# Moving the third group's attention norm and projections out of the first feed-forward and into the job list of attention

## The chip, the cores and the metric

The kernel runs on one core of a Trainium2 chip. The metric is the device time of one execution in microseconds, and lower is better. Three runs of the kernel before took 278.95, 279.00 and 279.03 us, a median of 279.0. The profiled execution took 278.83 us, of which the span from the first to the last instruction is 277.1 us; 1.73 us lie around the span.

## What is computed

A block of three layers on x of shape 2 x 1024 x 128 (2048 tokens, 128 features), all in float32:

```python
x = x + 0.5 * ffn(layernorm(x))        # 8 experts of 128 -> 256 -> 128, gelu, all experts, one gate factor per token
x = x + attention(layernorm(x))        # a second layer norm with weights inside; 8 heads of 8, q and k of unit length
x = x + 0.5 * ffn(layernorm(x))

# attention, for each batch row b (1024 tokens) and each head
xn = layernorm(x) * ln_w + ln_b
q, k, v = split(xn @ w_qkv)            # 128 -> 3 x 64
sim = 8 * l2norm(q) @ l2norm(k).T      # causal
out = softmax(sim) @ v @ w_out
```

## The kernel before, in words

**Tokens.** The 2048 tokens are four groups of 512 (`GROUPS`, `GROUP`), numbered 0 to 3; a group is four tiles of 128. Groups 0 and 1 are batch row 0, groups 2 and 3 are batch row 1. "The third group" is number 2, `LAST` is number 3.

**First feed-forward (layer 0).** `ffn_group(0, g)` runs 16 chunks `c` for each group (L561 on TensorE, L877 on ScalarE, L1121 on VectorE, L1400 on GpSimd). A chunk is three matmuls up (L524, L527, L530), a gelu on ScalarE (L849, often again as a rounded copy at L852), a split on VectorE (L1021, L1023) and three matmuls down (L542, L545, L547). The tables `AT...` (L67 to L81) say in which chunk each side task sits. While group `g` runs, the side tasks prepare attention for group `g - 1`: statistics and norm on VectorE (`normalise`, L962), transposes on TensorE (`ln_transpose`, L479), the affine copy on ScalarE (`affine_features`, L795), and the projection to q, k and v (`qkv_products`, L612). For group `g - 2`: squares, copies, inverse lengths by Newton steps, unit vectors, 16-bit stacks, and the transposes of the stacks to `qT` and `kT`.

**What group 3 of layer 0 (the fourth) does at its end.** Transposes of group 2's norm at chunk 12 (L485), `qkv_products(2)` at chunk 13 (L623), the first scores and exponentials of attention between the last chunks, and on VectorE at chunk 15 `copy_k(1)`, `copy_qkv(2)`, `own_squares(2)`, `square_sums(2)`, `guesses(2)` (L1184 to L1189). After this `y_transposes(3)` (L549) waits for `qkv_copied` of group 2, because it writes a PSUM bank that the q, k, v products used; `residual` for group 3 follows on VectorE (L1321).

**Attention.** There are 40 loops `k` (L739), each a pair of steps: `scores(2k)`, `scores(2k+1)` on TensorE (L655), two exponentials on ScalarE (L862), masks of diagonal blocks on GpSimd (L1462), and `pv(k - 3)` on TensorE (L678). Scores go through three sets of PSUM banks, so `scores(s)` waits until the exponential of step `s - 3` has read its set. The loops go through four query groups (called pairs in the code): loops 0 to 5, 6 to 19, 20 to 25 and 26 to 39. Loops whose step is the last of a unit (2, 5, 12, 19, 22, 25, 32, 39) are half as wide. Query group 2 (loop 20 on) needs `qT` and `kT` of token group 2, and query group 3 (loop 26 on) those of group 3.

**Jobs.** Work that must share TensorE with attention is a list `jobs` (L254) of (at, kind, argument). TensorE fills a job's PSUM bank right after `pv(at)` (L765), so in loop `at + 3`; `fill(n)` first waits until job `n - 1` has been emptied (L689), and everything behind it in TensorE's order waits with it. VectorE empties the jobs in order (`empty`, L1263) in the loop at L1328, and between them does the tasks hung on each job by name. With `q1` = 6, `q2` = 20, `q3` = 26 the list before is:

```python
jobs = [(q1, "ln", LAST), (q1 + 1, "project", (0, 0)), (q1 + 2, "project", (0, 1)),
        (q1 + 5, "qkv", 0), (q1 + 6, "qkv", 1), (q1 + 7, "q_stack", LAST - 1), (q1 + 8, "k_stack", LAST - 1),
        (q1 + 12, "q_stack", LAST), (q2 + 1, "k_stack", LAST),
```

`output(pair)` (L1244) is VectorE's reading of a finished query group; it waits for that group's last `pv`. `inverse_lengths` (L359) is nine small dependent instructions for groups 2 and 3, `unit_vectors` (L383) two, `stacks` (L1106) four.

**Second feed-forward (layer 1).** It follows attention and is not touched.

Of the kernel before, what the change touches and what calls it, by code (L numbers as in the profile page):

```python
# [34 lines left out]
GROUP_TILES = 4  # L35
# [25 lines left out]
Q_GROUPS = SEQ // GROUP  # L61
TURNS = 2 * (GROUPS - 1)
# [41 lines left out]
def build(nc, x, ln_w, ln_b, w_qkv, w_out, gate_w, gate_b, rms_w, w1, b1, w2, b2, out):  # L104
# [9 lines left out]
    with ctx:  # L114
# [125 lines left out]
        for st in steps:  # L240
# [13 lines left out]
        jobs = [(q1, "ln", LAST), (q1 + 1, "project", (0, 0)), (q1 + 2, "project", (0, 1)),  # L254
                (q1 + 5, "qkv", 0), (q1 + 6, "qkv", 1), (q1 + 7, "q_stack", LAST - 1), (q1 + 8, "k_stack", LAST - 1),
                (q1 + 12, "q_stack", LAST), (q2 + 1, "k_stack", LAST),
# [86 lines left out]
        def qkv_banks(p):  # L343

            return (BANK_LN, BANK_QT) if p == LAST - 1 else (BANK_QT, BANK_KT)
# [37 lines left out]
        def unit_vectors(eng, p):  # L383
            if p < LAST:
                eng.wait_ge(qkv_copied, p + 1)
            else:
                eng.wait_ge(job_emptied, job_number["qkv", 1] + 1)
# [90 lines left out]
        def _(pe):  # L478
# [82 lines left out]
            def ffn_group(layer, g):  # L561
# [5 lines left out]
                for c in range(CHUNKS):  # L567
# [26 lines left out]
                    if operands and g >= 1 and c == at["att_transpose"]:  # L594
# [14 lines left out]
                    if operands and g >= 1 and c == at["att_qkv"]:  # L609
                        qkv_products(g - 1)  # L610

            def qkv_products(p):  # L612
# [3 lines left out]
                if p == LAST - 1:  # L616
                    pe.wait_ge(qT_done, p)
                else:
                    pe.wait_ge(gate_logits_done, p + 2)
                    pe.wait_ge(qT_done, p)  # L620
                    pe.wait_ge(kT_done, p)
# [37 lines left out]
            def pv(k):  # L659
# [6 lines left out]
                if opens and pair == 0:  # L666
                    pe.wait_ge(kT_done, LAST - 1)
# [16 lines left out]
            def fill(n):  # L684
# [11 lines left out]
                elif kind in ("ln", "ffn_ln"):  # L696
                    norm = ATT if kind == "ln" else FFN
                    pe.wait_ge(xn_done[norm], GROUP_TILES * (LAST + 1 if kind == "ln" else GROUPS + 1))
                    for i, tile in enumerate(tiles):
                        m = pe.transpose(bank[:, tile], xn[:, norm, i, :], ident[:, :])  # L700
                elif kind == "qkv":
                    for i in halves[arg]:
# [36 lines left out]
            for k in range(quad_steps + PV_LAG):  # L739
                if k < quad_steps:  # L740
# [37 lines left out]
        def _(act):  # L778
# [98 lines left out]
            def ffn_group(layer, g):  # L877
# [5 lines left out]
                for c in range(CHUNKS):  # L883
# [23 lines left out]
                    if operands and g >= 1 and c == at["att_copy"]:  # L907
# [37 lines left out]
        def _(dve):  # L945
# [142 lines left out]
            def copy_qkv(p):  # L1088
                dve.wait_ge(qkv_mm, p + 1)
                dve.wait_ge(qkn_done, 2 * p)  # L1090
                halves_qkv = [ps[:, bank, 0:384].rearrange("p (t c) -> p t c", t=2) for bank in qkv_banks(p)]
                for half, qkv in enumerate(halves_qkv):
                    dve.tensor_copy(qk_raw[:, 2 * half:2 * half + 2, :], qkv[:, :, 0:2 * INNER])
                for half, qkv in enumerate(halves_qkv):
                    for quad in range(QUADS):
                        last = dve.tensor_copy(v_of(slice(4 * p + 2 * half, 4 * p + 2 * half + 2), quad), v_columns(qkv, quad))
                last.then_inc(qkv_copied, 1)

            def own_squares(p):
                if p == LAST:  # L1100
                    dve.wait_ge(job_emptied, job_number["qkv", 1] + 1)
                else:
                    dve.wait_ge(qkv_copied, p + 1)
# [17 lines left out]
            def ffn_group(layer, g):  # L1121
# [7 lines left out]
                for c in range(CHUNKS):  # L1129
# [133 lines left out]
            def empty(n):  # L1263
# [9 lines left out]
                elif kind == "ln":  # L1273
                    dve.wait_ge(qkv_mm, LAST)
                    dve.tensor_scalar(xf[:, ATT, :], bank, cols[:, COL_LNW:COL_LNW + 1], cols[:, COL_LNB:COL_LNB + 1],
                                      ALU.mult, ALU.add).then_inc(job_emptied, 1)
                elif kind == "qkv":
                    dve.wait_ge(qkn_done, 2 * LAST)
                    qkv = bank[:, 0:384].rearrange("p (t c) -> p t c", t=2)
                    t0 = GROUP_TILES * LAST + halves[arg][0]  # L1280
# [210 lines left out]
```

## Time and profile before

| what | value |
|---|---|
| median of three runs | 279.0 us |
| profiled execution, its span | 278.83 us, 277.1 us |
| TensorE busy (matmul) | 266.6 us (96%) |
| ScalarE busy | 220.8 us (80%) |
| VectorE busy | 220.1 us (79%) |
| GpSimd busy | 76.2 us (27%) |
| first feed-forward | from the start to about 113 us |
| attention | about 109 to 180 us |
| granted TensorE clock | 1.000 over the span |

The shares are means over three layers with different limits; a stage has to be read by itself. In the rows of the trace, the first number is the start in us from the span's start, the second is how long the merged group of instructions took, and the bracket at the end is how long the engine had been idle and what ended the wait. A group that is not merged with the next still overlaps it a little: the step from one start to the next is what an instruction costs its engine.

### The profile page before, as it was taken

How to read it: one execution, taken by the hardware profiler on the slowest of the kernel's cores; microseconds unless marked ns; L12 is line 12 of the kernel's file. 1: busy time of each engine (PE TensorE's matmuls, PEld its weight loads, DVE VectorE, ACT ScalarE, POOL GpSimd, SP SyncE). 2: the span in 40 equal slices, each digit the busy share in tenths (PEclk: the TensorE clock that was granted, in tenths of full speed). 3: DMA queues.
4: the chain of work that ended last, by engine and by line, in shares of the span. 5: the costliest groups of instructions: out<-in, count | busy, mean ns of one | idle time of the engine just before them, and what ended most of it. 6: DMA issues, size and time to landing. Idle time of an engine off the chain costs nothing.

```text
span 277.1 us, 4946 instructions
## 1 busy us (share of the span) xinstructions
PE 266.6 (96%) x1627; PEld 182.1 (66%) x1627; DVE 220.1 (79%) x597; ACT 220.8 (80%) x343; POOL 76.2 (27%) x148
## 2 busy tenths in 40 slices
PE   8999999999999999899998999999999999999994
PEld 8676778887778787323333432277876887888782
DVE  7799989998988988966687355587988797687775
ACT  2888677868888788899999999977685868668672
POOL 7103004213850482452347332600400200200100
PEclk9999999999999999999999999999999999999999
DMA  4740000000000000000000000420004210301302
GB/s 154 211 114 1 0 1 2 0 1 0 2 1 0 5 0 0 2 0 2 1 2 0 4 0 2 102 52 0 1 1 114 39 38 2 77 2 36 78 1 76
DMA packets 21644, 7.80 MB, mean 28 GB/s; under 512 B 13458, under 2 KB 20852, under 8 KB 21620
## 3 DMA queue, kind: packets, MB, share of 16 engines
q1 hardware_dynamic: 21620, 7.50, 10.5%
q8 instruction: 13, 0.21, 0.3%
q14 instruction: 11, 0.09, 0.1%
HBM read 4.88 MB, written 2.62 MB: 27 GB/s over the span
## 4 chain that ended last, share of the span: by engine, by line
PE 75%; DVE 10%; ACT 7%; issue 7%; DVEq 0%; POOL 0%; ACTq 0%; POOLq 0%
PE ps L547 9%; PE ps L530 9%; PE ps L542 9%; PE ps L524 9%; PE ps L527 9%; PE ps L678 9%; PE ps L545 8%; ACT probs L862 4%; PE ps L655 3%; DVE h_lo L1023 2%; PE ps L717 2%; PE ps L709 2%; PE ps L633 1%; DVE h_hi L1021 1%; ACT h_hi L852 1%
## 5 line engine op out<-in xcount | busy, mean ns | idle before, releaser
L849 ACT ACTIVATE h<-ps,cols 128x512 f32<-128x512 f32 x128 | 87.9, 692 | 43.3 <-PE ps L530 40.1
L1023 DVE TENSOR_TENSOR h_lo<-h,h_hi 128x512 fp32r<-128x512 f32 x128 | 89.1, 701 | 17.5 <-ACT h_hi L852 15.0
L862 ACT ACTIVATE probs<-ps 128x1024 f32<-128x1024 f32 (+1 forms) x80 | 67.3, 1008 | 1.6 <-PE ps L655 1.4
L542 PE MATMUL ps<-h_hi,w_hi 128*128 128x512 f32 x128 | 52.2, 408 | 0.3 <-DVE h_hi L1021 0.3
L547 PE MATMUL ps<-h_lo,w_hi 128*128 128x512 f32 x128 | 51.1, 399 | 0.8 <-DVE h_lo L1023 0.7
L524 PE MATMUL ps<-xT_hi,w_hi 128*128 128x512 f32 x128 | 50.6, 396 | 0.0
L530 PE MATMUL ps<-xT_lo,w_hi 128*128 128x512 f32 x128 | 50.1, 392 | 0.2 <-DVE xT_lo L381 0.2
L852 ACT ACTIVATE h_hi<-ps,cols 128x512 fp32r<-128x512 f32 x73 | 49.9, 684 | 0.0
L545 PE MATMUL ps<-h_hi,w_lo 128*128 128x512 f32 x128 | 49.9, 390 | 0.0
L527 PE MATMUL ps<-xT_hi,w_lo 128*128 128x512 f32 x128 | 49.9, 390 | 0.0
L678 PE MATMUL ps<-probs,v_ones 128*32 128x512 f32 (+3 forms) x384 | 38.8, 495 | 0.3 <-POOL probs L1462 0.2
L1462 POOL TENSOR_SCALAR_AFFINE_SELECT probs<-probs 128x256 f32<-128x256 f32 x64 | 25.7, 428 | 34.3 <-ACT probs L862 33.4
L1372 POOL TENSOR_TENSOR gate_rms<-gate_ms,neg_half 128x4 f32<-128x4 f32 x8 | 10.6, 1321 | 82.6 <-DVE gate_ms L988 82.6
L547 PEld LDWEIGHTS ps<-h_lo,w_hi 128*128 128x128 f32 x128 | 24.0, 188 | 9.7 <-DVE h_lo L1023 5.0
L542 PEld LDWEIGHTS ps<-h_hi,w_hi 128*128 128x128 f32 x128 | 24.0, 188 | 7.0 <-issue 1.8
L1021 DVE CAST h_hi<-h 128x512 fp32r<-128x512 f32 x55 | 23.1, 421 | 6.3 <-ACT h L849 5.7
L530 PEld LDWEIGHTS ps<-xT_lo,w_hi 128*128 128x128 f32 x128 | 24.0, 188 | 6.0 <-DVE xT_lo L381 0.6
L524 PEld LDWEIGHTS ps<-xT_hi,w_hi 128*128 128x128 f32 x128 | 24.1, 188 | 5.1 <-issue 0.6
L527 PEld LDWEIGHTS ps<-xT_hi,w_lo 128*128 128x128 f32 x128 | 24.0, 188 | 5.0
L545 PEld LDWEIGHTS ps<-h_hi,w_lo 128*128 128x128 f32 x128 | 24.1, 188 | 4.2
L655 PE MATMUL ps<-qT,kT 32*128 32x512 f16 (+3 forms) x192 | 20.8, 329 | 2.5 <-ACT probs L862 2.1
L655 PEld LDWEIGHTS ps<-qT,kT 32*128 32x128 f16 x192 | 6.2, 91 | 24.4 <-ACT probs L862 15.2
(147 smaller groups left out, 265.9 us busy)
## 6 DMA issues: line engine op xcount, KB each, us to landing
w_raw<-in_L_ffn_w SPq DMA_DIRECT2D x8, 256.0 KB, 3.8
turned<-blocks SPq DMA_DIRECT2D x6, 256.0 KB, 2.0
w_raw<-turned SPq DMA_DIRECT2D x24, 64.0 KB, 2.4
x_sb<-in_L_attn_x SPq DMA_DIRECT2D x3, 256.0 KB, 7.4
out_x<-x_sb SPq DMA_DIRECT2D x3, 256.0 KB, 2.3
x_sb<-in_L_attn_x SPq DMA_DIRECT2D x2, 128.0 KB, 2.2
out_x<-x_sb SPq DMA_DIRECT2D x2, 128.0 KB, 1.9
wout_sb<-in_L_attn_w_out SPq DMA_DIRECT2D x8, 4.0 KB
```

The lines of the kernel that those rows point to most:

```text
L524: pe.matmul(bank, w1_hi[:, w], xT_hi[:, cols_g], start=True, stop=False)
L527: pe.matmul(bank, w1_lo[:, w], xT_hi[:, cols_g], start=False, stop=False)
L530: pe.matmul(bank, w1_hi[:, w], xT_lo[:, cols_g], start=False, stop=True).then_inc(up_done, 1)
L542: pe.matmul(y, w2_hi[:, w], h_hi[:, c % RING, :], start=(c == 0), stop=False)
L545: pe.matmul(y, w2_lo[:, w], h_hi[:, c % RING, :], start=False, stop=False)
L547: pe.matmul(y, w2_hi[:, w], h_lo[:, c % RING, :], start=False, stop=(c == CHUNKS - 1)).then_inc(down_done, 1)
L655: m = pe.matmul(ps[:, 2 * score_set(s) + hd, at:at + width], kT[rows, st["quad"], k0:k0 + P], qT[rows, st["quad"], qc:qc + width], start=T ...
L678: m = pe.matmul(ps[ROW * j:ROW * j + ROW, bank, q0:q0 + width], v_ones[:, SEQ // P * st["b"] + kt, 4 * st["quad"] + j, :], probs[:, (s + j ...
L849: first = nc.scalar.activation(h[:, slot, :], ps[:, BANK_H + slot, :], ACT.Gelu, bias=bias)
L852: nc.scalar.activation(h_hi[:, slot, :], ps[:, BANK_H + slot, :], ACT.Gelu, bias=bias).then_inc(gelu_done, 1)
L862: nc.scalar.activation(probs[:, s % P_SLOTS, :, 0:width], ps[:, bank:bank + 2, 0:width], ACT.Exp, scale=SCALE).then_inc(exp_done, 1)
L1023: dve.tensor_tensor(h_lo[:, slot, :], h[:, slot, :], h_hi[:, slot, :].bitcast(f32), ALU.subtract).then_inc(split_done, 1)
```

## The change

Group 2's share in attention leaves group 3 of the first feed-forward. `FIRST_JOB = 2` is the first token group whose norm transposes, affine copy and q, k, v products are jobs. Its statistics and `normalise` on VectorE stay where they are. In group 3 of layer 0 there is no `ln_transpose(ATT, 2)`, no `affine_features(2)` and no `qkv_products(2)`, and VectorE's block at chunk 15 keeps only `copy_k(1)`. The job list begins with group 2's ln and two qkv halves at `q1`, then the two output projections of query group 0 (two places later than before), then group 3's ln (six later), the stacks of group 2 (same place), group 3's qkv halves (four later), and group 3's q stack (one later). On VectorE, group 2's squares, sums and guesses hang on its second qkv job; its inverse lengths, unit vectors and stacks all hang on the second projection job; group 3's squares, sums, guesses, inverse lengths, unit vectors and stacks all hang on its second qkv job; `normalise(ATT, 3)` moves from ahead of `output(0)` to behind the first job, and `first_stats` of the second feed-forward hangs on group 3's ln job. The number of instructions for the arithmetic stays nearly the same; q, k and v of group 2 are now copied by job halves.

```diff
+FIRST_JOB = 2
@@ jobs
-        jobs = [(q1, "ln", LAST), (q1 + 1, "project", (0, 0)), (q1 + 2, "project", (0, 1)),
-                (q1 + 5, "qkv", 0), (q1 + 6, "qkv", 1), (q1 + 7, "q_stack", LAST - 1), (q1 + 8, "k_stack", LAST - 1),
-                (q1 + 12, "q_stack", LAST), (q2 + 1, "k_stack", LAST),
+        jobs = [(q1, "ln", 2), (q1 + 1, "qkv", (2, 0)), (q1 + 2, "qkv", (2, 1)),
+                (q1 + 3, "project", (0, 0)), (q1 + 4, "project", (0, 1)), (q1 + 6, "ln", LAST),
+                (q1 + 7, "q_stack", 2), (q1 + 8, "k_stack", 2), (q1 + 9, "qkv", (LAST, 0)), (q1 + 10, "qkv", (LAST, 1)),
+                (q1 + 13, "q_stack", LAST), (q2 + 1, "k_stack", LAST),
                 (q2 + 4, "project", (1, 0)), (q2 + 5, "project", (1, 1)),
...
@@ TensorE, y_transposes of the last group
-                    pe.wait_ge(qkv_copied, LAST)
+                    pe.wait_ge(qkv_copied, FIRST_JOB)
+                    pe.wait_ge(qT_done, 2)
@@ TensorE, ffn_group
-                    if operands and g >= 1 and c == at["att_transpose"]:
+                    if operands and 1 <= g <= FIRST_JOB and c == at["att_transpose"]:
...
-                    if operands and g >= 1 and c == at["att_qkv"]:
+                    if operands and 1 <= g <= FIRST_JOB and c == at["att_qkv"]:
                         qkv_products(g - 1)
@@ TensorE, pv and the attention loop
-                    pe.wait_ge(kT_done, LAST - 1)
+                    pe.wait_ge(kT_done, 2)
+                    pe.wait_ge(gate_logits_done, GROUPS)
...
-                            pe.wait_ge(qkv_copied, LAST)
+                            pe.wait_ge(resid, GROUP_TILES * LAST)
+                            pe.wait_ge(xf_done[ATT], FIRST_JOB)
                             pe.wait_ge(y_evac, GROUPS)
@@ ScalarE, ffn_group
-                    if operands and g >= 1 and c == at["att_copy"]:
+                    if operands and 1 <= g <= FIRST_JOB and c == at["att_copy"]:
                         affine_features(g - 1)
@@ VectorE, normalise
-                if n <= GROUPS:
+                if kind == ATT and n > FIRST_JOB:
+                    dve.wait_ge(job_filled, job_number["ln", n - 1] + 1)
+                elif n <= GROUPS:
                     dve.wait_ge(ln_t[kind], n)
@@ VectorE, ffn_group, chunk 15 of the last group
                         copy_k(g - 2)
-                        copy_qkv(g - 1)
-                        own_squares(g - 1)
-                        square_sums(g - 1)
-                        guesses(g - 1)
@@ VectorE, the job loop
-            inverse_lengths(dve, LAST - 1)
-            normalise(ATT, LAST, LAST)
             for n, (at, kind, arg) in enumerate(jobs[:-1]):
                 if n == 0 or pair_of_job(n) != pair_of_job(n - 1):
                     output(pair_of_job(n) - 1)
                 empty(n)
-                if kind == "ln":
-                    unit_vectors(dve, LAST - 1)
+                if (kind, arg) == ("ln", 2):
+                    normalise(ATT, LAST, LAST)
+                if (kind, arg) == ("qkv", (2, 1)):
+                    own_squares(2)
+                    square_sums(2)
+                    guesses(2)
                 if (kind, arg) == ("project", (0, 1)):
-                    stacks(LAST - 1)
-                    dve.wait_ge(job_emptied, n + 1)
+                    inverse_lengths(dve, 2)
+                    unit_vectors(dve, 2)
+                    stacks(2)
+                if (kind, arg) == ("ln", LAST):
                     first_stats(GROUPS)
-                if (kind, arg) == ("qkv", 1):
+                if (kind, arg) == ("qkv", (LAST, 1)):
                     own_squares(LAST)
                     square_sums(LAST)
-                if (kind, arg) == ("q_stack", LAST - 1):
                     guesses(LAST)
-                if (kind, arg) == ("k_stack", LAST - 1):
                     inverse_lengths(dve, LAST)
                     unit_vectors(dve, LAST)
                     stacks(LAST)
```

## Rows read from the trace of the kernel before

**Rows 1.** Busy time by stretch: us; PE, PEld, DVE, ACT, POOL busy (x); PEclk, DMA
```profile
127.00:142.00 15.00, 15.00 (x154) 5.90 (x156) 9.76 (x30) 14.86 (x18) 4.17 (x9) 1.00 0.01 2
```
**Rows 2.** Timeline of ScalarE: start, us, line, operation, count, idle before
```profile
107.06 0.77 ACT L798 ACTIVATE xf<-ps,cols 128x512 f32<-128x512 f32 x1
...
110.16 0.22 ACT L839 ACTIVATE gate_tanh<-gate_tmp 128x32 f32<-128x32 f32 x1
...
111.87 1.03 ACT L862 ACTIVATE probs<-ps 128x1024 f32<-128x1024 f32 x1 [0.58 <-PE ps L655]
...
114.79 33.62 ACT L862 ACTIVATE probs<-ps 128x512 f32<-128x512 f32 x40 [0.41 <-PE ps L655]
148.79 29.87 ACT L862 ACTIVATE probs<-ps 128x512 f32<-128x512 f32 x36 [0.38 <-PE ps L655]
```
**Rows 3.** Timeline of TensorE at the end of the first feed-forward
```profile
106.27 0.60 PE L485 MATMUL ps<-ident,xn 128*128 128x128 f32 x4
...
109.23 1.57 PE L623 MATMUL ps<-wqkv_sb,xf 128*128 128x192 f32 x8
...
113.91 0.63 PE L558 MATMUL ps<-ident,yT 128*128 128x128 f32 x4 [0.86 <-DVE v_ones L1096]
```
**Rows 4.** Timeline of VectorE, end of the first feed-forward and start of attention
```profile
109.53 0.19 DVE L999 TENSOR_TENSOR gate_tmp<-logits,gate_max 128x32 f32<-128x32 f32 x1
...
112.50 0.75 DVE L1093 COPY qk_raw<-ps 128x256 f32<-128x256 f32 x2
...
113.87 0.69 DVE L1104 TENSOR_TENSOR sq<-qk_raw 128x512 f32<-128x512 f32 x1
...
116.06 1.12 DVE L1058 SCALAR_TENSOR_TENSOR x_sb<-ps,gate_half,x_sb 128x128 f32<-128x128 f32 x4
...
118.42 0.19 DVE L366 TENSOR_TENSOR newton<-rnorm 128x64 f32<-128x64 f32 x1
...
119.96 0.37 DVE L366 TENSOR_TENSOR newton<-rnorm 128x64 f32<-128x64 f32 x1
...
120.98 1.52 DVE L967 TENSOR_SCALAR xn<-x_sb,mean_var,rstd 128x128 f32<-128x128 f32 x4
```
**Rows 5.** Timeline of GpSimd beside that
```profile
119.84 2.94 POOL L1462 TENSOR_SCALAR_AFFINE_SELECT probs<-probs 128x256 f32<-128x256 f32 x8
```
**Rows 6.** Timeline of VectorE, from the first finished query group on
```profile
124.36 0.72 DVE L1247 STREAM_TRANSPOSE o_blocks<-ps 128x512 f32<-128x512 f32 x1 [1.86 <-PE ps L678]
...
127.17 0.81 DVE L1275 TENSOR_SCALAR xf<-ps,cols 128x512 f32<-128x512 f32 x1 [0.51 <-PE ps L700]
```
**Rows 7.** Timeline of TensorE in attention: score, pv and job pieces of loops 10 to 15
```profile
128.39 0.71 PE L709 MATMUL ps<-wout_sb,o_feat 128*128 128x128 f32 x4
...
131.22 1.06 PE L678 MATMUL ps<-probs,v_ones 128*32 128x512 f32 x8
132.22 0.39 PE L655 MATMUL ps<-qT,kT 32*128 32x512 f16 x4
132.54 1.07 PE L678 MATMUL ps<-probs,v_ones 128*32 128x512 f32 x8
...
136.79 0.92 PE L703 MATMUL ps<-wqkv_sb,xf 128*128 128x192 f32 x4
```
**Rows 8.** Timeline of VectorE: group 3's copies, squares, Newton steps and stacks
```profile
137.75 0.42 DVE L1281 COPY qk_raw<-ps 128x256 f32<-128x256 f32 x1 [1.06 <-PE ps L703]
...
138.54 0.69 DVE L1104 TENSOR_TENSOR sq<-qk_raw 128x512 f32<-128x512 f32 x1
...
142.11 0.38 DVE L366 TENSOR_TENSOR newton<-rnorm 128x64 f32<-128x64 f32 x1
...
145.22 0.76 DVE L392 TENSOR_TENSOR qkn<-qk_raw,rnorm 128x256 f32<-128x256 f32 x2
...
147.16 0.62 DVE L409 TENSOR_TENSOR k_stack<-qkn,k_stack 128x256 f16<-128x256 f32 x1
```
**Rows 9.** Timeline of TensorE: group 3's q stack job in loop 21
```profile
147.93 0.61 PE L633 MATMUL ps<-ident,q_stack 128*128 128x128 f16 x8 [0.82 <-DVE k_stack L409]
```

More of the change, by code:

```diff
@@ L343, in qkv_banks @@
         def qkv_banks(p):
-            return (BANK_LN, BANK_QT) if p == LAST - 1 else (BANK_QT, BANK_KT)
+            return BANK_QT, BANK_KT
         def stack_words(stack):
@@ L383, in unit_vectors @@
         def unit_vectors(eng, p):
-            if p < LAST:
+            if p < FIRST_JOB:
                 eng.wait_ge(qkv_copied, p + 1)
             else:
-                eng.wait_ge(job_emptied, job_number["qkv", 1] + 1)
+                eng.wait_ge(job_emptied, job_number["qkv", (p, 1)] + 1)
             if p:
@@ L615, in qkv_products @@
                 pe.wait_ge(xf_done[ATT], p + 1)
[L616 to L621, printed above, removed]
+                pe.wait_ge(gate_logits_done, p + 2)
+                pe.wait_ge(qT_done, p)
+                pe.wait_ge(kT_done, p)
                 for i in range(GROUP_TILES):
@@ L697, in fill @@
                     norm = ATT if kind == "ln" else FFN
-                    pe.wait_ge(xn_done[norm], GROUP_TILES * (LAST + 1 if kind == "ln" else GROUPS + 1))
+                    pe.wait_ge(xn_done[norm], GROUP_TILES * (arg + 1 if kind == "ln" else GROUPS + 1))
                     for i, tile in enumerate(tiles):
@@ L701, in fill @@
                 elif kind == "qkv":
-                    for i in halves[arg]:
+                    for i in halves[arg[1]]:
                         m = pe.matmul(bank[:, 192 * (i % 2):192 * (i % 2) + 192], xf[:, ATT, tiles[i]], wqkv_sb[:, :],
@@ L1086, in copy_k @@
                                 ps[:, BANK_KT, :].bitcast(f16).rearrange("p (a q) -> p a q", a=QUADS)).then_inc(kT_done, 1)
[L1088 to L1097, printed above, removed]
             def own_squares(p):
[L1100 to L1103, printed above, removed]
+                dve.wait_ge(job_emptied, job_number["qkv", (p, 1)] + 1)
                 dve.tensor_tensor(sq[:, :, :], qk_raw[:, :, :], qk_raw[:, :, :], ALU.mult).then_inc(sq_done, 2)
@@ L1273, in empty @@
                 elif kind == "ln":
-                    dve.wait_ge(qkv_mm, LAST)
+                    if arg == FIRST_JOB:
+                        dve.wait_ge(qkv_mm, FIRST_JOB)
+                    else:
+                        dve.wait_ge(job_filled, job_number["qkv", (arg - 1, 1)] + 1)
                     dve.tensor_scalar(xf[:, ATT, :], bank, cols[:, COL_LNW:COL_LNW + 1], cols[:, COL_LNB:COL_LNB + 1],
@@ L1277, in empty @@
                 elif kind == "qkv":
-                    dve.wait_ge(qkn_done, 2 * LAST)
+                    p, half = arg
+                    dve.wait_ge(qkn_done, 2 * p)
                     qkv = bank[:, 0:384].rearrange("p (t c) -> p t c", t=2)
-                    t0 = GROUP_TILES * LAST + halves[arg][0]
-                    dve.tensor_copy(qk_raw[:, halves[arg][0]:halves[arg][1] + 1, :], qkv[:, :, 0:2 * INNER])
+                    t0 = GROUP_TILES * p + halves[half][0]
+                    dve.tensor_copy(qk_raw[:, halves[half][0]:halves[half][1] + 1, :], qkv[:, :, 0:2 * INNER])
                     for quad in range(QUADS):
```

## The prediction

> **What bounds the kernel now.** I read the busy time by stretch first, then ScalarE's timeline, because attention is the stage that receives the work. From 127 to 142 us ScalarE is busy 14.86 of 15 us and TensorE 15.00 of 15 [rows 1]: neither has room, and VectorE has 9.76. ScalarE's exponentials run in two almost unbroken stretches, 40 in 33.62 us and 36 in 29.87 us [rows 2]. The second holds 28 full and 8 half-width ones; with 0.91 us for a full and 0.48 us for a half one it is 29.3 us, so these are the paces, and the first (32 full, 8 half) should take 33.0: about 0.6 us of it are small waits for TensorE. So attention ends when 80 exponentials have been fed. Whatever makes TensorE late with scores for longer than its lead makes the kernel longer by that much, one for one.
>
> Next, TensorE's rhythm [rows 7]. A full pv takes 1.00 us (131.22 to 132.22) and a full pair of scores 0.32 (132.22 to 132.54), so a loop costs TensorE 1.32 us against 1.81 for ScalarE: 0.49 of slack, and a job longer than that eats the lead. In a half-width loop (scores about 0.22, pv of three loops before 1.00) TensorE needs 1.22 against 0.96: it loses even without a job. The lead is at most three score sets, since scores(s) waits for exponential s - 3.
>
> Last, the one place where the chain already leaves ScalarE: group 3's q stack job waits 0.82 us for VectorE's last stack instruction [rows 9], and ScalarE idles 0.38 us right behind it [rows 2]. VectorE's chain to that point starts at 137.75 with group 3's copies and ends at 147.16 + 0.62 = 147.78 [rows 8]. That is 10.0 us from the qkv job to the stacks, and the old list leaves six loops for it (job in loop 15, q stack in loop 21). This chain decides the case.
>
> **Part 1, the end of the first feed-forward: a gain of 1.4 us.** Removed are the four transposes (0.60 us long), the q, k, v products (1.57) [rows 3] and the affine copy, 0.77 us [rows 2]. ScalarE's table load and first exponential move up by about 0.8, but the tanh behind them needs the gate values that VectorE finishes at 109.53 + 0.19 = 109.72 [rows 4] whatever is removed, against a start at 110.16 [rows 2]: 0.4 remains. The exponential at 111.87 had waited 0.58 for scores behind the products [rows 2]; they are gone, so it follows its predecessor and the gain is 1.0. The transposes of y at 113.91 waited 0.86 for VectorE's copy of v [rows 3], and the exponential at 114.79 waited 0.41 for scores behind them [rows 2]. Both waits vanish, since only ScalarE's own evacuation of y is left in front: gain 1.0 + 0.4 = 1.4. Next to be late there is ScalarE itself. The new waits in this place (qT of group 1, residuals, the gate's logits) are for things finished before that, so they cost nothing.
>
> On VectorE, 3.6 us leave the boundary (112.50 to 116.06) [rows 4], so group 3's residual starts at about 113.2. Residual, statistics and aggregation took 116.06 to 118.42, hence they end near 115.5. Then VectorE has nothing until query group 0 is finished. That moment was 124.36 [rows 6] and moves with ScalarE to about 122.95. The old kernel filled this hole with the Newton steps (118.42 to 120.98) and the norm of group 3 (1.52) [rows 4]. The new one leaves it empty and does both later. Idle VectorE time costs nothing, but this work now stands in the job chain.
>
> **Part 2, loops 9 to 15.** I follow TensorE by its starts, in the new kernel's time. In the old one the job behind pv in loop 10 started at 128.39 [rows 7], with one ln job before it as in the new; minus 1.4, the first qkv half starts at 127.0. A record of a job overlaps the next by some 0.07 (a pv is 1.06 long and its next starts after 1.00), so a qkv half is 0.85 (0.92 less 0.07), a projection 0.64 (0.71 less 0.07) [rows 7], an ln or a stack 0.6 [rows 3, 9]. So: qkv ends 127.85; loop 11 with pv 129.15; second qkv half 130.0; loop 12 (half-width) 131.25; projection 131.9; loop 13 133.2. Meanwhile VectorE had the second half's copies, 0.8 [rows 8], then squares, sums and guesses, 2.2 (113.87 to 116.06) [rows 4], to 133.05, and only then empties the projection, at 133.4. The second projection's fill waits for that and ends at 134.0. Loops 14 and 15 have slack and no heavy job; pv of loop 15 ends at 136.5 and group 3's ln fill at 137.1, then TensorE finishes pv of loop 16 at 138.8. In this stretch the exponentials lose about 1.9 us (0.3, 0.3, 1.0 and 0.3 in loops 11 to 14), against some 0.5 of the old kernel's 0.6.
>
> **Part 3, the first stall.** Group 2's q stack job in loop 16 may be filled only when group 3's ln is emptied, and in VectorE's order that stands behind Newton steps, unit vectors and stacks of group 2. From the second projection emptied at 134.45: Newton 2.3, unit vectors and stacks 2.55 (145.22 to 147.78) [rows 8], emptying ln 0.7 (0.81 less overlap) [rows 6]: 140.1. TensorE was ready at 138.8, so it waits 1.4, and exponential 34 comes 1.3 late. The 2.3 for nine Newton steps is a choice: six took 1.54 (118.42 to 119.96), 0.26 each, the next three 1.02 [rows 4], when GpSimd had begun its masks at 119.84 [rows 5]; group 3's nine took 3.1 beside masks [rows 8]. At this place no diagonal block is near, so I take the quick pace. The Trainium skill ("SBUF — State Buffer", section Who interferes with whom) has a two-input VectorE instruction contend with GpSimd's reads, which the slower steps beside the masks agree with; without that rule the whole Newton would be 3.1 and the sum 0.8 larger.
>
> **Part 4, loops 17 to 20.** q stack fill ends 140.75; loop 17 142.1; k stack 142.7; loop 18 144.05; qkv of group 3 144.9; half-width loop 19 146.1; second qkv half 147.0. Two 0.85 jobs around a half-width loop put scores of loop 20 at 147.3 where ScalarE could have taken them at 146.2. Lost here: 0.1 + 0.3 + 1.2 = 1.6.
>
> **Part 5, the second stall, the largest term.** Group 3's second qkv half is now filled in loop 19 and its q stack in loop 22: three loops instead of six. VectorE needs copies 0.8, squares, sums and guesses 2.2 [rows 4, 8], and from the first Newton step to the last stack 5.67 (142.11 to 147.78) [rows 8]: 8.65 us. From 147.05 this ends at 155.7, and the fill starts at 155.85 (the old one started 0.15 behind its chain [rows 8, 9]). TensorE has finished pv of loop 22 by about 152. ScalarE has exponentials 40 to 45 in hand, 4 x 0.91 + 2 x 0.48 = 4.6 us from 147.4, so it is empty at 152.0. The next, 46, needs the fill and its scores: the old exponential 44 came 0.86 behind the fill's start [rows 2, 9], a full one needs 0.1 more, so 156.8. Lost: 4.8 us.
>
> **The sum.** The old exponential 46 started at 148.79 + 2 x 0.48 = 149.75 [rows 2], the new one at 156.8: +7.05. (By terms: -1.4 + 1.9 + 1.3 + 1.6 + 4.8 = 8.2, less 1.1 of old waits up to there.) Behind it the k stack job meets loop 24 a little tighter, +0.15. The rest of attention has the same jobs in the same loops, and with ScalarE unbroken for 29.87 us [rows 2] there is no slack to win back; the second feed-forward only shifts. So +7.2 on the profiled 278.83 gives 286.0 us. That execution lies 0.2 below the median of 279.0, within what I can resolve. About 0.2% is what a measurement of this kernel can tell from no change.
>
> **Rivals.** First, faster. If group 3's stacks were ready when TensorE reaches loop 22, only the boundary's 1.4 would count, and the time is 278.8 - 1.4 = 277.4. This decides at a chain of 4.6 us (exponentials 40 to 45) plus the lead, some 5 us. Against it stands 10.0 us for the same instructions in the old trace [rows 8], 8.65 without the two stack copies between them. Chance 0.04; something near no change, by several shorter chains at once, 0.03.
>
> Second, a smaller loss: TensorE keeps its lead up to loop 19, because VectorE's chain of group 2 is hidden and the fills cost less than their records. Then pv of loop 19, whose old time is about 1.4 us later than the new, ends near 142.8; with 0.85 and 8.65 and the 1.1 to exponential 46 it starts at 153.5: +3.7, so 282.5. For it speaks that job fills in the merged rows overlap their neighbours; against it TensorE's 15.00 of 15 us [rows 1]. Between this and the forecast lies 282.5 to 284.3; chance 0.17.
>
> Third, TensorE's clock. It was granted in full in the stretch shown [rows 1], where TensorE never idled; a wait of 4 us as in part 5 is in none of the rows. If the clock falls from 2.4 to 1.2 GHz there, a loop costs 2.64 against ScalarE's 1.81, losing 0.83 each; two to four loops give +1.7 to +3.3, time 287.7 to 289.3. The Trainium skill ("TensorE: Matmul & The Clock Gate", section HAM oscillation) says that idle gaps of TensorE drop its clock to half, and by that rule the second stall is a candidate; no row here shows it. Chance 0.13.
>
> **How the numbers follow.** The forecast of 286.0, with its own spread of 284.3 to 287.7 (the 0.8 of the Newton pace upwards, 1.7 of fills and waits downwards), has 0.63. Slower in all: 0.63 + 0.17 + 0.13 = 0.93; same 0.03; faster 0.04. The range reaches from the second rival's end, 282.5, into the third, 288.6; beyond it are the first rival and part of the third.
>
> **What would show it.** In the changed profile: the exponential behind y's transposes near 113.4; VectorE idle about 7 us before 123; the first q stack job idle before it about 1.4 us, put down to VectorE's xf; group 3's q stack at about 155.9 with 3.5 to 4 us idle before it, put down to k_stack; ScalarE's stretch from there on 29 us long. It would be wrong if VectorE's chain from the group 3 qkv copies to its last stack were well under 8 us, or if ScalarE's idle time within attention summed to less than 5 us.

## The result and the profile after

The changed kernel takes 289.08 us, median of four runs (288.79 to 289.16), against 279.01 for the kernel before in the same session. The ratio is 1.0351, 95% interval 1.0336 to 1.0365: slower by 10.1 us. I had forecast 286.0 and a range of 282.5 to 288.6; the direction was right, the time lies 0.5 us outside the range. The profiled execution took 289.02 us, its span is 287.3 us (before: 277.1).

The page of the changed kernel, first the busy times and shares, then 40 slices of 7.2 us each; PEclk is the granted TensorE clock in tenths (9 stands for full):

```profile
PE 271.3 (94%) x1627; PEld 182.9 (64%) x1627; DVE 219.8 (77%) x598; ACT 221.0 (77%) x342; POOL 75.5 (26%) x148
...
PEclk9999999999999999799998699999999999999998
```

ScalarE, VectorE and GpSimd are busy within 0.7 us of what they were before (220.8, 220.1 and 76.2 us), so for them the span has grown by waiting. TensorE is busy 4.7 us longer (266.6 before), because its clock, full in every slice before, has two dents. By stretches of the changed kernel (us; busy time of PE, PEld, DVE, ACT, POOL; then the clock):

```profile
113.00:114.80 1.80, 1.29 (x12) 0.74 (x12) 1.08 (x4) 1.47 (x3) 0.96 (x3) 1.00 0.00 0
114.80:118.20 3.40, 3.40 (x26) 0.72 (x28) 1.30 (x9) 2.78 (x4) 2.48 (x6) 0.50 0.02 5
118.20:155.70 37.50, 31.68 (x316) 11.64 (x308) 23.07 (x72) 31.57 (x38) 13.28 (x33) 1.00 0.00 1
155.80:162.50 6.70, 5.50 (x44) 1.83 (x44) 3.73 (x8) 3.37 (x4) 1.15 (x3) 0.50 0.00 0
```

TensorE ran at 1.2 instead of 2.4 GHz for 3.4 us at the start of attention and for 6.8 us around group 3's q stack. The mean granted clock of the four executions was 0.976 to 0.980, so all four had it low for about as long.

ScalarE's timeline, which answers [rows 2]. One unbroken stretch of 40 exponentials and one of 36 have become many; each bracket is idle time of ScalarE in front of scores:

```profile
110.06 0.23 ACT L841 ACTIVATE gate_tanh<-gate_tmp 128x32 f32<-128x32 f32 x1 [0.17 <-DVE gate_tmp L1003]
...
113.94 2.92 ACT L864 ACTIVATE probs<-ps 128x512 f32<-128x512 f32 x4 [0.33 <-PE ps L655]
117.48 15.22 ACT L864 ACTIVATE probs<-ps 128x1024 f32<-128x1024 f32 x18 [0.62 <-PE ps L655]
133.58 1.94 ACT L864 ACTIVATE probs<-ps 128x1024 f32<-128x1024 f32 x2 [0.88 <-PE ps L655]
...
142.31 5.03 ACT L864 ACTIVATE probs<-ps 128x1024 f32<-128x1024 f32 x6 [0.95 <-PE ps L655]
148.43 4.75 ACT L864 ACTIVATE probs<-ps 128x1024 f32<-128x1024 f32 x6 [1.08 <-PE ps L655]
158.35 1.94 ACT L864 ACTIVATE probs<-ps 128x1024 f32<-128x1024 f32 x2 [5.17 <-PE ps L655]
161.07 1.94 ACT L864 ACTIVATE probs<-ps 128x1024 f32<-128x1024 f32 x2 [0.78 <-PE ps L655]
163.62 25.22 ACT L864 ACTIVATE probs<-ps 128x512 f32<-128x512 f32 x30 [0.61 <-PE ps L655]
```

TensorE's timeline at the two waits, which answers [rows 9]:

```profile
141.33 0.62 PE L633 MATMUL ps<-ident,q_stack 128*128 128x128 f16 x8 [1.28 <-DVE xf L1264]
...
156.76 1.01 PE L633 MATMUL ps<-ident,q_stack 128*128 128x128 f16 x8 [4.57 <-DVE k_stack L411]
...
158.55 1.94 PE L679 MATMUL ps<-probs,v_ones 128*32 128x512 f32 x8 [0.24 <-DVE qT L1255]
```

The first wait is for the emptying of group 3's ln, the second for group 3's last stack. The stack transposes behind it take 1.01 us where they took 0.61 before, and a pv 1.94 instead of 1.06: that is the low clock. VectorE, which answers [rows 6, 8]:

```profile
124.23 0.72 DVE L1233 STREAM_TRANSPOSE o_blocks<-ps 128x512 f32<-128x512 f32 x1 [8.06 <-PE ps L679]
...
140.47 0.80 DVE L1264 TENSOR_SCALAR xf<-ps,cols 128x512 f32<-128x512 f32 x1
...
148.10 0.42 DVE L1271 COPY qk_raw<-ps 128x256 f32<-128x256 f32 x1 [1.38 <-PE ps L704]
...
151.15 0.23 DVE L368 TENSOR_TENSOR newton<-rnorm 128x64 f32<-128x64 f32 x1
...
156.19 0.42 DVE L411 TENSOR_TENSOR k_stack<-qkn,k_stack 128x256 f16<-128x256 f32 x1
```

It idles 8.06 us until query group 0 is done, and the chain from 148.10 to 156.19 + 0.42 = 156.61 is 8.5 us long.

**A common mark.** Executions start differently: the first matmul of the first feed-forward began at 7.94 us before, at 8.26 after, and between 7.97 and 8.79 in the experiments. So I compare from a mark that all share, the start of the last gelu of the first feed-forward (106.47 before, 106.78 after):

```profile
106.78 0.69 ACT L851 ACTIVATE h<-ps,cols 128x512 f32<-128x512 f32 x1
```

Exponentials are numbered from 0 as in the prediction. All figures are us behind that mark, from ScalarE's timelines and the spans, each of one profiled execution; the last column is the end against the kernel before. (In q_late the q stack stands one loop later, so the wait for it comes behind exponential 46 and not ahead of it.)

| kernel | exponential 4 | exponential 20 | exponential 40 | exponential 46 | end | end against before |
|---|---|---|---|---|---|---|
| before | 8.32 | 21.10 | 38.14 | 43.29 | 170.62 | |
| changed | 7.16 | 20.71 | 41.65 | 51.57 | 180.49 | +9.87 |
| fill_late | 7.20 | 20.88 | 41.82 | 51.05 | 178.36 | +7.74 |
| fill_early | 6.88 | 19.66 | 40.64 | 50.58 | 178.84 | +8.22 |
| fill_both | 6.88 | 19.65 | 40.64 | 49.88 | 177.21 | +6.59 |
| short_chain | 7.16 | 20.57 | 41.47 | 48.45 | 177.21 | +6.59 |
| filled_short_second | 6.88 | 19.66 | 40.65 | 48.09 | 175.40 | +4.78 |
| filled_short_first | 6.88 | 19.66 | 39.29 | 48.53 | 175.86 | +5.24 |
| late_chain | 8.32 | 21.08 | 39.33 | 49.26 | 177.53 | +6.91 |
| late_chain_filled | 8.32 | 22.03 | 40.23 | 49.46 | 178.33 | +7.71 |
| q_late | 7.44 | 21.56 | 42.46 | 47.05 | 180.66 | +10.04 |
| hole | 7.16 | 20.99 | 38.10 | 43.26 | 170.61 | -0.01 |
| copyk_last | 8.13 | 20.91 | 37.95 | 43.10 | 170.44 | -0.18 |
| hole_early_filled | 6.88 | 20.63 | 37.74 | 42.88 | 170.20 | -0.42 |

### The profile page after: what moved, and what is told of

Its sections match the earlier page's. It is cut to its first block, busy times and chain, and to the rows that moved or that the text cites. A ratio compares the mean times of both kernels' runs of the same rounds, so it can differ in the third digit from the quotient of the medians.

```text
span 287.3 us, 4947 instructions
## 1 busy us (share of the span) xinstructions
PE 271.3 (94%) x1627; PEld 182.9 (64%) x1627; DVE 219.8 (77%) x598; ACT 221.0 (77%) x342; POOL 75.5 (26%) x148
## 4 chain that ended last, share of the span: by engine, by line
PE 71%; DVE 14%; issue 7%; ACT 7%; DVEq 0%; POOL 0%; ACTq 0%; POOLq 0%
PE ps L549 9%; PE ps L544 9%; PE ps L526 8%; PE ps L532 8%; PE ps L529 8%; PE ps L547 8%; PE ps L679 8%; ACT probs L864 4%; DVE h_lo L1027 3%; PE ps L655 3%; PE ps L718 2%; PE ps L710 1%; PE ps L633 1%; DVE h_hi L1025 1%; PE ps L704 1%
## 5 line engine op out<-in xcount | busy, mean ns | idle before, releaser
L864 ACT ACTIVATE probs<-ps 128x1024 f32<-128x1024 f32 (+1 forms) x80 | 68.2, 980 | 11.0 <-PE ps L655 10.7
L679 PE MATMUL ps<-probs,v_ones 128*32 128x512 f32 (+3 forms) x384 | 41.7, 528 | 0.3 <-DVE qT L1255 0.2
```

The source lines that it names most:

```text
L679: m = pe.matmul(ps[ROW * j:ROW * j + ROW, bank, q0:q0 + width], v_ones[:, SEQ // P * st["b"] + kt, 4 * st["quad"] + j, :], probs[:, (s + j ...
L864: nc.scalar.activation(probs[:, s % P_SLOTS, :, 0:width], ps[:, bank:bank + 2, 0:width], ACT.Exp, scale=SCALE).then_inc(exp_done, 1)
```

## The experiments

The theory after the result: the forecast's steps hold, and two falls of TensorE's clock come on top. The rivals: the falls cost nothing, since ScalarE has work in hand; and the loss is not the shortened distance of group 3's chain but group 2's work crowding loops 9 to 19. The "dummies" below are matmuls whose result nobody reads; they only keep TensorE working while it waits.

### What the clock costs: fill_late, fill_early, fill_both

```diff
 late, in fill(n), ahead of the wait for the stacks
+if (kind, arg) == ("q_stack", LAST):
+    for _ in range(12):
+        pe.matmul(bank[:, 0:P], ones[:, :], ones[:, :], start=True, stop=True)
 early, in y_transposes(LAST), ahead of the wait for y_evac
+for _ in range(4):
+    pe.matmul(ps[:, bank, 0:P], ones[:, :], ones[:, :], start=True, stop=True)
```

> The changed kernel with twelve dummy matmuls (128x128, into the job's own bank) in group 3's q stack job, between the wait for the job before and the wait for the stacks; nothing they write is read. Theory: the wait there is VectorE's and stays (q stack at about 156.8 us), but the dummies keep TensorE active, so its granted clock does not fall from 155.8 to 162.6 us as in the changed kernel's trace. The slow q stack (1.01 instead of 0.62 us) and the exponentials' waits of 0.89 and 0.73 us behind it go: 2.0 us, so 287.1 us, clock 0.988. Rival, the lower clock costs nothing because ScalarE has its work in hand: 289.1.

> The changed kernel with four dummy matmuls ahead of the transposes of y at the start of attention, where TensorE waits for ScalarE's evacuation (1.4 us). Theory: they keep the clock from falling at 114.8 to 118.2 us, the wait of 0.76 us ahead of exponential 8 goes, and about 0.8 to 1.0 us are won: 288.2. If four are too few to hold the clock, the time stays 289.1, and the trace shows the fall; if they delay the transposes it is up to 0.3 longer.

> Both fills. Theory: the two clock losses add: 289.1 - 2.0 - 0.9 = 286.2 us at a clock of 1.000, which is the time I had forecast without any fall of the clock (286.0). Rival: the second stall absorbs what the first fill wins, so it is the time of the late fill alone, 287.1.

Measured: fill_late 287.30 us (286.63 to 288.29), fill_early 287.48 (286.86 to 287.76), fill_both 286.79 (285.86 to 287.73). In the profiled executions the late fill leaves only the first fall, the early fill only the second (now from 153.5 to 160.3), and both together leave none (the clock of fill_both is full in every slice of its page). TensorE and ScalarE at the second wait of fill_both:

```profile
151.71 2.94 PE L699 MATMUL ps<-ones 128*128 128x128 f32 x24
156.28 0.62 PE L635 MATMUL ps<-ident,q_stack 128*128 128x128 f16 x8 [1.62 <-DVE k_stack L411]
```
```profile
157.26 8.44 ACT L869 ACTIVATE probs<-ps 128x1024 f32<-128x1024 f32 x10 [4.49 <-PE ps L657]
```

The q stack still waits for VectorE, its transposes take 0.62 instead of 1.01, and from exponential 46 on ScalarE has no pause for the two loops in which it had waited 0.78 and 0.61. Behind the mark the late fill wins 2.13 us, the early one 1.65, both 3.28 of the 9.87: 1.06 up to exponential 20 (20.71 against 19.65) and 2.2 behind it. Not all of it is the clock. At exponential 4, ahead of the first fall, the early fill has already won 0.28: the transposes of y start 0.05 us behind ScalarE's evacuation of y where they started 0.36 behind it in the changed kernel, and why is open. So the two falls cost about 3.0 us, 0.8 and 2.2, and the rival that the low clock is hidden falls.

In the medians the gain of both fills is smaller, 2.3 us, and the runs spread by 1.9. The mean granted clock, on record for every execution, shows why: in fill_both it was 0.998 and 0.997 in the two at 286.33 and 285.86 us, and 0.991 and 0.994 in the two at 287.25 and 287.73. The kernel before has 0.997 to 1.000 in all but one of the seven executions beside them, so in those two the dummies did not hold it. In fill_late it was 0.994 in two (286.63, 286.82) and 0.986 in two (287.78, 288.29). With the clock held the time is thus about 286.1, 3.0 below the changed kernel. Where the clock fell in executions that were not profiled is not known. The early fill won more than the 0.8 to 1.0 that I expected.

### The chain of group 3: short_chain, filled_short_second

```diff
 in inverse_lengths
+if p == LAST:
+    return
...
```

(The count of Newton steps that others wait for is lowered to match. The kernels of this part and the next leave a computation out, so their q and k are not the right ones.)

> The changed kernel without the nine Newton steps of group 3's inverse lengths (its q and k keep the rough first guess of their lengths, the rest is computed). It takes 3.1 us out of VectorE's chain between the second qkv job and the stacks. Theory, that chain sets the q stack: TensorE's wait falls from 4.6 to about 1.5 us, the clock no longer falls behind it, and 3.1 + 2.0 are won: 284.0 us. Rival, the wait is for something else or the loss is spread over all jobs: less than 1 us won, 288 or more.

> The kernel with both fills, without group 3's nine Newton steps (q and k of group 3 keep the rough first guess of their lengths). The run without fills left the chain 3 us shorter, but its clock fell behind the wait all the same. Theory: with the clock held, each us of chain is a us of time: exponential 46 comes 3.0 us sooner after the last gelu of the first feed-forward than with both fills (49.9 us), 46.9, and the time is 286.8 - 3.0 = 283.8. Rival, TensorE's backlog stands behind the chain: under 2 us won.

Measured: 286.91 us (285.96 to 287.68) and 284.21 (283.70 to 284.45). In short_chain TensorE's wait is 2.25 us, down from 4.57:

```profile
154.49 0.61 PE L635 MATMUL ps<-ident,q_stack 128*128 128x128 f16 x8 [2.25 <-DVE k_stack L413]
```

From exponential 40 to 46 it takes 6.98 us instead of 9.92: 2.94 won for 3.1 of chain, so this chain does set the q stack. The time stayed 2.9 us above my expectation, and the clock fell twice here too, from 115.6 to 119.0 and from 156.5 to 159.9; in two of the four executions its mean was lower still (0.973 against 0.985 and 0.986). In the filled form I expected 3.0 and found 1.8 at exponential 46. The reason is my own dummies: they start at 151.28 and take 2.94 us, and VectorE's last stack was ready at 152.84 + 0.62 = 153.46, so TensorE came to the job behind them:

```profile
151.28 2.94 PE L701 MATMUL ps<-ones 128*128 128x128 f32 x24
154.06 0.61 PE L637 MATMUL ps<-ident,q_stack 128*128 128x128 f16 x8
```

No idle bracket stands before the q stack, so this run shows only that at least 1.8 us hang on the chain; the unfilled pair is the cleaner measure. The clock was held in all four executions (0.998 to 1.000), and their median is 1.9 below the 286.1 of fill_both's two held ones.

### The chain of group 2: filled_short_first

```diff
 in inverse_lengths
+if p == 2:
+    return
```

> The kernel with both fills, without group 2's nine Newton steps (q and k of group 2 keep the rough guess). Theory: TensorE's first wait, 1.3 us ahead of group 2's q stack, goes, and as everything behind it follows from TensorE's own order, the whole 1.1 us that exponential 34 had lost reach the end: 285.6 us. Rival, the second wait takes it up: 286.8, and that wait is longer by 1.1.

Measured: 284.60 us (284.33 to 284.89). The first wait of TensorE is gone, exponential 40 comes 1.35 us sooner than in fill_both (39.29 against 40.64) and the end too (175.86 against 177.21). Nothing behind takes it up: the second wait is 1.61 behind the dummies as before. The forecast's first stall is real and reaches the end in full. The clock was held in all four executions (0.997 to 1.000), and their median is 1.5 below the 286.1 of fill_both's two held ones; that it is also 1.0 below my expectation comes in part from the two executions of fill_both in which the clock was not held.

### One part of the change alone: late_chain, late_chain_filled

```diff
 kernel before
-        (q1 + 5, "qkv", 0), (q1 + 6, "qkv", 1), (q1 + 7, "q_stack", LAST - 1), (q1 + 8, "k_stack", LAST - 1),
-        (q1 + 12, "q_stack", LAST), (q2 + 1, "k_stack", LAST),
+        (q1 + 7, "q_stack", LAST - 1), (q1 + 8, "k_stack", LAST - 1), (q1 + 9, "qkv", 0), (q1 + 10, "qkv", 1),
+        (q1 + 13, "q_stack", LAST), (q2 + 1, "k_stack", LAST),
```

> The kernel before with one part of the change alone: group 3's two qkv jobs at q1 + 9 and q1 + 10 (four loops later), its q stack at q1 + 13 (one later), and its guesses, Newton steps, unit vectors and stacks hung on the second qkv job. Group 2 stays in the first feed-forward. Theory, the shortened distance is the main cause: the qkv job then ends behind pv of loop 19 at about 145.0, the chain of 8.65 us ends at 153.7, the next exponential starts at about 154.9 against 149.75, +5.1; TensorE waits some 3 us, and if the clock falls, up to 1.5 more: 284.1 to 285.6 us. Rival, the loss comes from group 2's work crowding loops 9 to 19: then this kernel is within 1.5 us of 279.0.

> The kernel before with group 3's qkv jobs four loops later, with twelve dummy matmuls in its q stack job as in the late fill. In the run without them the clock was low from 152.0 to 158.8 us. Theory: the dummies hold it, and the chain alone is left: exponential 46 at 43.3 + 5.6 = 48.9 us behind the last gelu of the first feed-forward, 284.5 us in all. Rival: the dummies do not matter, 286.0.

Measured: 286.03 us (285.84 to 286.67) and 284.67 (284.30 to 287.39). The first is above the 284.1 to 285.6 that I had expected. Group 2 is where it always was, and yet 7.0 us are lost:

```profile
145.90 4.75 ACT L862 ACTIVATE probs<-ps 128x1024 f32<-128x1024 f32 x6 [1.07 <-PE ps L655]
155.83 1.94 ACT L862 ACTIVATE probs<-ps 128x1024 f32<-128x1024 f32 x2 [5.17 <-PE ps L655]
```
```profile
154.24 1.01 PE L633 MATMUL ps<-ident,q_stack 128*128 128x128 f16 x8 [4.57 <-DVE k_stack L409]
```

The two brackets, 1.07 and 5.17, are nearly those of the changed kernel (1.08 and 5.17), and so is TensorE's wait of 4.57. Exponential 46 is 5.97 us late behind the mark. About 0.7 of it is the low clock from 152.0 to 158.8: from exponential 40 to 46 it takes 9.93 us, and 9.24 in fill_both, where the clock was held. So the later place of group 3's jobs costs about 5.3 us by itself: 1.2 is there at exponential 40, from the qkv jobs around the half-width loop 19, and 4.1 more at exponential 46, from the distance of three loops between qkv and q stack. That is the main cause, and the rival falls, but the crowding is not nothing. In fill_both exponential 34 is 1.03 us late though the boundary had won 1.44, and in late_chain it is not late at all (33.42 against 33.49): group 2's jobs and the first wait cost 2.5 us up to there. With the clock held, the loss of fill_both at exponential 46 is thus -1.44 (boundary) + 2.47 (up to exponential 34) + 1.47 (to 40) + 4.09 (to 46) = 6.59 us. The fill gave 1.4 us in the medians, as expected (mean clock 0.997 to 1.000 in three executions, 284.30 to 285.02 us), but not in its profiled execution, which is the slowest of the four: there the clock fell at the start of attention, in code that is the same as in the kernel before, and again 1.5 us behind the start of the q stack:

```profile
116.30:119.70 3.40, 3.40 (x22) 0.64 (x26) 3.23 (x17) 2.61 (x4) 1.07 (x3) 0.50 0.02 5
...
157.30:160.60 3.30, 3.30 (x24) 0.65 (x28) 1.96 (x4) 2.30 (x3) 0.81 (x2) 0.50 0.00 0
```

Dummies are no sure means. The kernel before may have such a fall too: two of its later executions, 280.59 and 280.57 us, have a mean clock of 0.990 where the others have 0.996 to 1.000.

### One loop more: q_late

```diff
-                (q1 + 13, "q_stack", LAST), (q2 + 1, "k_stack", LAST),
+                (q2, "q_stack", LAST), (q2 + 1, "k_stack", LAST),
```

> The changed kernel with group 3's q stack job one loop later (at q2, loop 23), nothing else. Theory: the chain ends at the same time, but TensorE goes on for one loop more, so ScalarE has two more exponentials (1.8 us) in hand; TensorE's wait falls from 4.6 to about 3 us. VectorE's output of query group 1 now stands ahead of the q copy and gives about 1 back: 0.8 to 1.8 us won, and more if the clock stays up: 286 to 288 us. Rival, the k stack behind it becomes the late one and all is given back: 289.

Measured: 287.56 us (286.77 to 288.94), 1.5 less than the changed kernel. The profiled execution is again the slowest: it wins nothing (+10.04 at the end), and its clock was low twice for 6.8 us. The two executions with the higher mean clock (0.991) took 286.77 and 287.09, the other two (0.976, 0.979) 288.94 and 288.03. Its rows show both halves of the trade:

```profile
158.20 1.01 PE L633 MATMUL ps<-ident,q_stack 128*128 128x128 f16 x8 [3.50 <-DVE o_blocks L1233]
161.56 1.03 PE L633 MATMUL ps<-ident,k_stack 128*128 128x128 f16 x8
```

The wait falls from 4.57 to 3.50, but it now ends with VectorE's output of query group 1, and the k stack follows closely. With the clock so different I take no figure from it beyond the median.

### Where group 2's work could go: hole, hole_early_filled, copyk_last

Between the start of attention and query group 0's end VectorE has 8 us, and PSUM bank 6 is free until loop 9 once the last residual has read it. So group 2's jobs can be done there.

```diff
+        jobs = [(1, "ln", 2), (2, "qkv", (2, 0)), (3, "qkv", (2, 1)),        # hole
+        jobs = [(0, "ln", 2), (1, "qkv", (2, 0)), (3, "qkv", (2, 1)),        # hole_early_filled, with the early fill
                 (q1, "ln", LAST), (q1 + 1, "project", (0, 0)), (q1 + 2, "project", (0, 1)),
                 (q1 + 5, "qkv", (LAST, 0)), (q1 + 6, "qkv", (LAST, 1)), (q1 + 7, "q_stack", 2), (q1 + 8, "k_stack", 2),
                 (q1 + 12, "q_stack", LAST), (q2 + 1, "k_stack", LAST),
...                                # VectorE's tasks and the wait of pv move with the jobs
+                if n == 0:
+                    pe.wait_ge(resid, GROUP_TILES * GROUPS)
 kernel before, copyk_last
+                        copy_qkv(g - 1)
                         copy_k(g - 2)
-                        copy_qkv(g - 1)
```

> Group 2's ln and two qkv jobs in loops 4, 5 and 6, into the bank that is free until query group 1 opens, so that VectorE does them and group 3's norm in the 8 us in which the changed kernel leaves it idle; all other jobs in the loops of the kernel before, Newton steps of group 2 behind its first projection job. Theory, the loss is all in the job list and the boundary's gain is real: the q stack is back at about 147, no wait of TensorE over 1 us in attention, 278.0 to 279.0 us. Rival, TensorE has no room for 2.3 us more before loop 9 either: 280 or more.

> Group 2's jobs in loops 3, 4 and 6 instead of 4, 5 and 6 (the half-width loop 5 gets none), and four dummy matmuls ahead of the transposes of y to hold the clock. In the first such kernel exponentials 12 and 14 came 0.67 and 0.34 us late. Theory: they come 0.4 us late in all, the boundary's gain of 1.2 to 1.4 is kept to two thirds, and with the same start as the kernel before it is 278.2 us. Rival, the 2.3 us of TensorE work find no room anywhere ahead of loop 9 and the gain is eaten: 279.0 or, with a later start, up to 279.9.

> The kernel before with one swap on VectorE at the end of the first feed-forward: group 2's q, k, v copies ahead of the copy of group 1's k, which is not read before loop 6. TensorE's transposes of y waited 0.86 us for these copies. Theory: they come 0.4 us earlier, then wait for ScalarE's evacuation, and 278.7 us results. Rival, the exponential behind them or VectorE's later start gives it back: 279.0.

Measured: hole 280.64 us (279.75 to 281.62), ratio 1.0052 (1.0031 to 1.0073). Its waits behind the boundary are the old ones:

```profile
120.74 1.94 ACT L866 ACTIVATE probs<-ps 128x1024 f32<-128x1024 f32 x2 [0.49 <-PE ps L655]
122.91 26.36 ACT L866 ACTIVATE probs<-ps 128x1024 f32<-128x1024 f32 x30 [0.23 <-PE ps L655]
...
148.78 0.61 PE L633 MATMUL ps<-ident,q_stack 128*128 128x128 f16 x8 [0.82 <-DVE k_stack L411]
```

In this execution all of the 9.87 us are gone (end at 170.61 behind the mark, before 170.62): they were in the list, not in the idea of the jobs. The gain of the boundary, 1.16 at exponential 4, is eaten by the waits ahead of exponentials 12 and 14, so the rival that TensorE has no room ahead of loop 9 has the better of my 278.0 to 279.0. The profiled execution started 0.85 later than that of before (8.79 against 7.94), which is its 279.75. The other four were longer still (280.52 to 281.62), and their mean clock was 0.994 in three and 0.988 in the slowest, against 0.998 in the profiled one: a fall of the clock is the likely reason, though where it fell was not traced.

hole_early_filled: 278.67 us (278.57 to 279.37, 12 runs), ratio 0.9981 (0.9970 to 0.9992) against the kernel before, whose runs of that session have a median of 279.28. It is 10 us faster than the changed kernel, and faster than the kernel before by an amount at the edge of what can be told. Its mean clock was 0.996 to 1.000 in all 12 executions. At the end it is 0.42 ahead behind the mark: of 1.44 at exponential 4, 1.0 is lost to the group 2 jobs by exponential 20, more than the 0.4 that I expected. copyk_last: 278.91 us, ratio 0.9995 (0.9986 to 1.0004), no change that can be told, though exponential 4 is 0.19 sooner.

## Why the forecast was right and wrong

**What bounds the kernel** held: attention is paced by ScalarE, and each us by which scores came late reached the end. fill_both and filled_short_first show it one for one (1.35 us at exponential 40 and at the end).

**The step that failed.** The sum has no term for TensorE's clock. Part 1 priced the removed waits as pure gain, and part 5 sized a wait of 4 us and left what could come of it to a rival. The runs showed two falls of the clock in its place, about 3.0 us: 0.8 at the boundary, which no part and no rival had, and 2.2 at the second wait. The books close on the profiled executions: 289.02 is 2.99 above 278.83 + 7.2, and 3.28 (what both fills win back, with the 0.28 of quicker transposes) less 0.61 (the sum was 7.2 and fill_both measured +6.59) plus 0.31 (the later mark) is 2.98. Without the fall at the boundary the time is in the range: fill_early, whose profiled execution has only the second, took 286.86 to 287.76 us.

**Part 1, the boundary, 1.4:** in the changed kernel itself 1.16 (exponential 4 at 7.16 against 8.32), since the transposes of y started 0.36 us behind ScalarE's evacuation; with the early dummies 1.44 (6.88). By exponential 20 only 0.39 of it was left in the changed kernel (20.71 against 21.10) and all of it in fill_both (19.65). I did not ask what TensorE would do in the time set free. It waits 1.40 us in one piece for that evacuation, where in the kernel before it waited 0.86 for VectorE [rows 3]:

```profile
113.06 0.63 PE L561 MATMUL ps<-ident,yT 128*128 128x128 f32 x4 [1.40 <-ACT yT L876]
```

By stretches, the kernel before and then the changed one, TensorE worked 4.00 of 4 us between 109 and 113 and now 2.65, all of the difference being that wait (the 0.86 of before came just behind this stretch),

```profile
109.00:113.00 4.00, 4.00 (x24) 2.50 (x24) 3.08 (x12) 3.41 (x7) 0.86 (x3) 1.00 0.00 0
```
```profile
109.00:113.00 4.00, 2.65 (x16) 1.20 (x14) 2.57 (x11) 3.83 (x6) 1.59 (x4) 1.00 0.00 0
```

and its clock fell at 114.8. The page TensorE: Matmul & The Clock Gate of the Trainium skill, section HAM oscillation, has the clock fall after long idle gaps. The trace doesn't bear that out for this fall, where no gap of TensorE was over 1.40 us, and it does for the second one, at 155.8, when TensorE had been idle since 152.19.

**Part 2, loops 11 to 14, 1.9 us late:** 1.8 by the exponentials' starts (late by 0.25, 0.24, 0.99 and 0.34). **Part 3, the first stall, 1.4 of TensorE and 1.3 at exponential 34:** 1.28 and 1.12. The quick Newton pace was the right choice: nine steps from 135.77 to 138.06, 2.3 us, and GpSimd's last mask was over at 133.50. **Part 4, 0.1 + 0.3 + 1.2:** 0.06, 0.24 and 1.20.

**Part 5, the second stall, 4.8:** 4.65 with the clock held, 5.34 in the changed kernel, where the stack transposes and the scores behind them ran at the low clock. The chain was 8.5 us, forecast 8.65.

**The sum, +7.2:** +6.59 in fill_both, which has dummies of its own. The steps were sized to within 0.3 us each, mostly a little too large. The first two rivals fall: the second stall is there, and the lead was not kept up to loop 19 (exponential 40 is 2.5 us late in fill_both).

**The third rival came true, beside the forecast and not instead of it.** I gave 1.7 to 3.3 us for a fall behind the second wait, and it was 2.2. What was wrong in it is the chance, 0.13, and the range that followed from it: I took "no row here shows it" for evidence against, when the kernel before had simply never let TensorE idle for over 1 us in attention. Seen from here, a wait of 4 us forecast by my own sum should have made the fall the likelier case, and 288 the forecast.

**Not settled:** when exactly the clock falls. It fell 1.0 us ahead of the end of the 4.6 us wait in one execution and 2.7 ahead in another (fill_early), behind a wait of 2.25 (short_chain), and once in a stretch where the code was that of the kernel before (late_chain_filled), with no gap over 0.86 us ahead of it. In the profiled execution of hole the boundary has a gap of 1.41 us and the clock did not fall. So the same code can have a fall or not, which fits the wider spread of the changed lists; the moment was traced for one execution of each kernel only.

## What to carry to other kernels

Measure a chain that crosses engines from its first instruction to its last, count the loops that the list leaves it, and compare: 8.5 us of VectorE's chain against 4.6 us of ScalarE's work in hand was most of the case. Work moved "to where there is room" has to go where the engine that is last in its chain has room; here VectorE's 8 us ahead of query group 0 were room, the loops behind it were not. And where a sum contains an idle TensorE of some us, put the lower clock into the forecast, not into the rivals.

## What the runs showed of the hardware

The granted clock fell at the boundary without any gap over 1.4 us in front of it, after a stretch in which TensorE was busy 2.65 of 4 us, and in one execution (late_chain_filled) without any over 0.86; in another (hole) it stayed full behind a gap of 1.41. It stayed low for 3.4 us in some places and 6.8 in others, and in the low stretches a pv took 1.94 us instead of 1.06. Such a stretch cost less than its length: the one of 3.4 us 0.8, the one of 6.8 us between 1.6 (fill_early against fill_both) and 2.1 (changed against fill_late). The start of an execution moves too: the first feed-forward's first matmul came between 7.94 and 8.79 us, latest (8.60 to 8.79) in the four executions in which the kernel's own twelve dummies at the start took 5.49 us (4.80 in the kernel before), so two single executions should be compared from a mark behind it.
